# Holding five tiles of the last sequence back behind the last keys, moving their running sums to GpSimd, and reordering the work from the attention's biases to the end

## The reference

```
x = x + xattn(ln(x), ctx)     # 16 heads x 128; q, k = rmsnorm(x Wq), rmsnorm(ctx Wk); softmax(q k / sqrt(128)) (ctx Wv) Wo
x = x + attn(ln(x))           # 16 heads x 32, causal inside a sequence; qkv = x W + b, output W_proj + b
x = x + ffn(ln(x))            # silu(gate) * up, rms_norm, ternary weights: gate_up 512 -> 2 x 2048, proj 2048 -> 512
```

## Time and profile before

| | |
|---|---|
| three runs | 1558.96, 1561.87, 1562.70 us, median 1561.87 |
| profiled execution | 1560.27 us, its span 1558.4 us |
| mean granted TensorE clock | 0.985 of 2.4 GHz |
| TensorE busy | 1490.0 us, 96% of the span |
| VectorE, ScalarE, GpSimd busy | 1248.6, 970.6, 162.8 us |

### The profile page before, as it was taken

One profiled execution on the slowest core, in us unless ns is written; L12 is line 12 of the kernel. 1 busy time (PEld: TensorE's weight loads), 2 busy tenths in 40 slices (PEclk: granted clock), 3 DMA queues, 4 the chain that ended last, 5 costly groups with the idle time before them and its releaser, 6 DMA issues.

```text
span 1558.4 us, 21889 instructions
## 1 busy us (share of the span) xinstructions
PE 1490.0 (96%) x6860; PEld 1200.9 (77%) x6896; DVE 1248.6 (80%) x1952; ACT 970.6 (62%) x3637; POOL 162.8 (10%) x121
## 2 busy tenths in 40 slices
PE   7989999999999999999999999999999977987998
PEld 5767778888888888888888888888888855885786
DVE  6647878988898988899889889888988876768443
ACT  4666667767676767677667676776666654613332
POOL 2210000002000200110020002000202011022342
PEclk9999999999999999999999999999999988998999
DMA  5532221211221111112112111111110154450000
GB/s 175 172 116 71 68 70 45 65 42 32 78 68 35 60 58 60 43 57 67 51 31 80 56 46 55 58 46 39 51 30 20 44 178 135 149 217 1 1 0 28
DMA packets 86467, 105.19 MB, mean 67 GB/s; under 512 B 7240, under 2 KB 67664, under 8 KB 85328
## 3 DMA queue, kind: packets, MB, share of 16 engines
q1 hardware_dynamic: 79056, 96.46, 19.5%
q10 hardware_dynamic: 7296, 7.34, 1.4%
HBM read 81.24 MB, written 22.54 MB: 67 GB/s over the span
## 4 chain that ended last, share of the span: by engine, by line
PE 79%; DVE 13%; ACT 4%; issue 3%; DMA 1%; another core or an unknown queue 0%; POOL 0%; ACTq 0%; POOLq 0%; DVEq 0%
PE ps L36 25%; PE ps L37 24%; PE ps L38 24%; DVE ring L977 2%; PE ps L756 2%; PE ps L757 2%; ACT ps L1462 1%; DVE p_lo L42 1%; PE ps L774 1%; PE ps L775 1%; DVE ring L948 0%; ACT recip L1498 0%; DVE q_rstd L879 0%; DMA wq_raw<-in_wq 0%; DVE w_q L1062 0%
## 5 line engine op out<-in xcount | busy, mean ns | idle before, releaser
L1462 ACT ACTIVATE ps<-ps 123x128 f32<-123x128 f32 (+1 forms) x1248 | 325.5, 261 | 136.3 <-PE ps L38 135.5
L36 PE MATMUL ps<-wk_hi,cT_hi 128*128 128x512 f32 x832 | 330.1, 397 | 7.6 <-ACT ps L1462 4.4
L37 PE MATMUL ps<-wk_lo,cT_hi 128*128 128x512 f32 x832 | 326.9, 393 | 0.0
L38 PE MATMUL ps<-wk_hi,cT_lo 128*128 128x512 f32 x832 | 324.5, 390 | 0.0
L1462 ACT ACTIVATION_READ_ACCUMULATOR ps<-ps 123x1 f32 (+1 forms) x1248 | 231.1, 185 | 0.0
L36 PEld LDWEIGHTS ps<-wk_hi,cT_hi 128*128 128x128 f32 x832 | 156.4, 188 | 51.2 <-ACT ps L1462 10.7
L38 PEld LDWEIGHTS ps<-wk_hi,cT_lo 128*128 128x128 f32 x832 | 156.7, 188 | 34.4
L36 PE MATMUL ps<-p_hi,cn_hi 123*128 123x512 f32 (+1 forms) x416 | 173.2, 416 | 10.3 <-DVE p_lo L42 10.3
L37 PEld LDWEIGHTS ps<-wk_lo,cT_hi 128*128 128x128 f32 x832 | 157.0, 189 | 31.7
L37 PE MATMUL ps<-p_lo,cn_hi 123*128 123x512 f32 (+1 forms) x416 | 165.6, 398 | 0.0
L36 PE MATMUL ps<-fq_hi,cT_hi 128*128 128x512 f32 x416 | 162.2, 390 | 1.9 <-DVE fq_lo L42 1.9
(11 more groups left out here) (222 smaller groups left out, 2676.9 us busy)
## 6 DMA issues: line engine op xcount, KB each, us to landing
cT_raw<-in_ctxT SPq DMA_DIRECT2D x96, 128.0 KB, 3.5
cn_raw<-in_ctx SPq DMA_DIRECT2D x88, 123.0 KB
w_raw<-in_wguT SPq DMA_DIRECT2D x32, 256.0 KB, 2.7
qk_scratch<-folded ACTq DMA_DIRECT2D x8, 896.0 KB, 4.2
fq_raw<-qk_scratch SPq DMA_DIRECT2D x14, 512.0 KB, 3.7
pc_scratch<-pc_out SPq DMA_DIRECT2D x7, 1024.0 KB, 4.2
ternary_scratch<-w_out SPq DMA_DIRECT2D x48, 128.0 KB, 1.7
w_bf<-ternary_scratch SPq DMA_DIRECT2D x1, 6144.0 KB, 22.7
```

What stands on the lines that cost most here:

```text
L36: pe.matmul(dst, l_hi, r_hi, start=first, stop=False)
L37: pe.matmul(dst, l_hi, r_lo, start=False, stop=False)
L38: return pe.matmul(dst, l_lo, r_hi, start=False, stop=last)
L1462: done = act.activation(head, head, ACT.Square, accum_out=k_sum[0:n, i, g * GH + h:g * GH + h + 1])
```

## The change

1. **Steps.** The last key steps take one slot each; the program's loop ends at step N-1 = 103. Five tiles of the first part (94 to 98) have their context matmuls behind the last keys and scores, in a tail written out tile by tile; `cn_hi`/`cn_lo` get three buffers.
2. **GpSimd** takes the running sums of tiles 94 to 98 and the rescaling of the sum.
3. **Newton first.** Behind the last `key_mean` VectorE does `key_refine`, scale and maximum at once.
4. **End by halves of heads.** The sums, the reciprocal (`last_guess`, `last_refine`), the last tile's context (`last_context`) and `add_parts` go by half (8 heads); `divide_parts` of groups 1 to 3 lies in the head loop.
5. **Value loop.** Output matmuls are two heads behind (three `oT`, four `wo` buffers); the last three heads are ordered by token tile.
6. **Attention.** `qk_bias` goes to ScalarE; `low_wa(2, .)` lies ahead of `causal_shifted(1)`; `attend(m)` alternates banks 6 and 0.
7. **Feed-forward.** Gate and up of slice 1 for the first 256 tokens fill the place behind the last `z_turn`; the last slice's squares go to TensorE directly.

```diff
-        per_step = [0] * (TT + 1) + [1] * (LAST - TT) + [1, 1, 2, 2, 2, 2, 2, 1] + [1, 1, 2, 2, 2]
+        per_step = [0] * (TT + 1) + [1] * (LAST - TT) + [1, 1, 2, 2, 2, 2, 2, 1] + [1, 1, 1, 1]
+        HELD = slots_done[-1]
...
+        SUB_IN = {LAST: [LAST], LAST + 1: [LAST + 1], LAST + 2: [LAST + 2, LAST + 3], LAST + 3: [LAST + 4, LAST + 5]}
+        EXP_IN = {LAST: [LAST], LAST + 1: [LAST + 1], LAST + 2: [LAST + 2, LAST + 3], LAST + 3: [LAST + 4]}
...
+            def last_context():
+                v, n = N - 1, tiles[N - 1][2]
+                pe.wait_ge(p_lo_done, N)
+                denominators(v)
+                pe.wait_ge(cn_lo_done, N)
+                for half in range(2):
+                    hh = slice(half * BANK, (half + 1) * BANK)
+                    for c2 in range(KC):
+                        cc = slice(c2 * P, (c2 + 1) * P)
+                        done = products(pe, bank(PART_AV_BANK + c2 * 2 + half), cn_hi[0:n, v % 3, cc],
+                                        cn_lo[0:n, v % 3, cc], p_hi[0:n, v % 2, hh], p_lo[0:n, v % 2, hh], False, True)
+                    done.then_inc(av_mm, 1)
...
+            for half in range(2):
+                scores(N - 1, half)
+            for v in range(HELD - 1, N - 1):
+                for c2 in range(KC):
+                    weighted_context(v, c2)
+            last_context()
...
-                heads = [head - 1] if 1 <= head < H - 1 else [H - 2, H - 1] if head == H else []
+                late = range(H - NH3, H)
+                parts = [(m, [head - 2]) for m in range(MT)] if 2 <= head < H - 1 else [
+                    (0, late[:2]), (1, late[:2]), (0, late[2:]), (1, late[2:]), (2, late), (3, late)] if head == H else []
...
-                            pe.wait_ge(v_biased, MT)
-                            if m > 0:
-                                pe.wait_ge(aT_lo_done, m)
+                            pe.wait_ge(v_biased, max(m + 1, MT - 1))
+                            if m == 1:
+                                pe.wait_ge(causal_scaled, 4 * MT)
+                            elif m > 1:
+                                pe.wait_ge(aT_lo_done, m - 1)
...
             z_turn(MT - 1)
+            gate_or_up(1, 0, 0, 2)
+            gate_or_up(1, 1, 0, 2)
...
-            pe.wait_ge(h_sq_added, FT)
+            pe.wait_ge(h_sq_added, FT - 1)
+            pe.wait_ge(h_squared, FT)
...
+                pe.matmul(bank(7)[:, m:m + 1], sq_sum[:, cols], ones_col[:], start=True, stop=False)
+                done = pe.matmul(bank(7)[:, m:m + 1], h_sq[:, (FT - 1) % 2, cols], ones_col[:], start=False, stop=True)
...
-            sum_refine(B - 1)
-            add_parts()
-            evacuate(B - 1)
-            low_pc(0)
-            low_pc(1)
+            last_refine(0)
+            add_parts(0)
+            divide_parts(0)
+            add_parts(1)
+            low_pc(0)
+            add_parts(2)
+            add_parts(3)
+            low_pc(1)
+            last_refine(1)
...
+            def track_sum(u):
+                n = tiles[u][2]
+                pool.wait_ge(exped, u + 1)
+                pool.wait_ge(summed, sum_count(u - 1))
+                pool.tensor_tensor(run_sum[0:n], run_sum[0:n], ring[0:n, u % RING], ALU.add).then_inc(summed, 1)
+            track_sum(HELD - 1)
+            track_sum(HELD)
+            pool.wait_ge(maxed, max_count(N - 1))
+            pool.wait_ge(fq_lo_done, KC * B)
+            pool.partition_all_reduce(fq_raw[:], run_max[:], P, bass.bass_isa.ReduceOp.max).then_inc(max_spread, 1)
+            for u in range(HELD + 1, LAST + PART):
+                track_sum(u)
...
+            pool.tensor_tensor(run_sum[:], run_sum[:], col_max[:], ALU.mult).then_inc(sum_split, 1)
...
+            load_cn(HELD + 2)
+            sp.wait_ge(scores_mm, N)
+            sp.wait_ge(w_stored, 16 * NP)
+            load_v_weights(0)
+            load_v_weights(1)
+            for s in range(HELD + 3, N):
+                load_cn(s)
```

442 lines of the change are left out of this document (244 added, 198 removed).

## The result

The changed kernel takes 1548.28 us, median of 4 runs (1547.17 to 1548.97), against 1561.24 us of the kernel before, median of 4 on the same chip. The ratio is 0.9918, with a 95% interval of 0.99 to 0.9935: faster by 13 us. The profiled execution took 1548.61 us, 11.7 less than the one before; its span of 1545.9 is 12.5 shorter. So half of the forecast gain is missing, and the rest of this text looks for it.

What follows compares the result with a forecast made beforehand. TensorE, busy 1490.0 of 1558.4 us, bounds the kernel; only seams, mostly waits for VectorE with low clock behind long ones, can be won. Gains 11 + 1 + 1.5 + 8 + 2.5 + 1 = 25 us give 1535.3 us, range 1523 to 1549.

Steps and rivals of the forecast that it cites:

- B: Values: gain of 1 us (-1 to 3), with new small waits for the second and third head.
- C: Start of the attention: the 2.3 us wait shrinks by 0.7 us to all of it; gain 1.5 us (0.5 to 2.5).
- A: Tail, last keys to values: values start earlier; gain 11 us (3 to 20).
- Step 3: Tail, maximum to last `p_lo`: VectorE's own instructions take 24.5 us together.
- step 4: Tail: GpSimd and VectorE stand in each other's way, costing VectorE 10.2 us, 1.7 of them for the all-reduce.
- step 6: Tail: takes off 2 us for slow-clock matmuls behind remaining waits and 1 us for SP's queue.
- D: Attention: waits for `wa_lo` and `aT_lo` go, with the first's low clock; gain 8 us (4 to 10).
- E: Feed-forward start: 16 matmuls fill the 1.5 us wait and some clock comes back; gain 2.5 us (1 to 4).
- F: End: the 1.5 us wait for the last GpSimd addition goes, four one-column matmuls come; gain 1 us (0.5 to 1.5).
- rivals, 2: Tail, values and attention: gaps and low clock stay, the tail gains 3 us less; 1546 us, chance 0.19.
- Rival 3: Attention: the wait only changes its name, to `causal_scaled` and `p_diag`; gain there 2 us, 1541 us; chance 0.09.
- Rival 4: Tail: a GpSimd library load ahead of the all-reduce gates the maximum; 1571 us at a 30 us load; chance 0.05.

Runs made afterwards that it cites:

- Experiment 1: Changed kernel with the three divisions of groups 1 to 3 all behind the first head instead of one behind each of heads 1 to 3; 1544.19 us.
- experiments 1 and 2: The changed kernel with early divisions (1544.19 us), and the changed kernel with block 2's weights widened ahead of the loop over the feed-forward's slices (1548.23 us).
- Experiment 13: Experiment 11's kernel with the 16 query and key biases back on VectorE, in the order from before the change; 1541.78 us.
- Experiment 10: Experiment 6's kernel with all of attend's products in bank 6 again, as before the change; 1535.49 us.
- Experiment 11: Experiment 6's kernel with the old end: GpSimd adds the last slice's squares and TensorE multiplies only the sum; 1533.17 us.
- experiment 4: Changed kernel with context tiles 98 and 99 loaded ahead of the value and output weights in SP's queue; 1543.96 us.
- experiment 8: Experiment 5's kernel with two small GpSimd probe instructions, directly ahead of and behind the all-reduce; 1543.7 us.
- experiment 6: Experiment 5's kernel with block 2's weights widened ahead of the loop over the feed-forward's slices; 1535.14 us.
- experiment 5: Changed kernel with the running sums and rescaling back on VectorE and the three divisions behind the first head; 1536.39 us.
- kernels 5 to 12: The kernel with sums on VectorE and early divisions, and variants built on it; medians 1533.2 to 1536.4 us without the one with GpSimd probes.

## Why the prediction was wrong, step by step

**B is the step that failed most.** The prediction prices the values by the small waits of the second and third head and calls them a gain of 1 us. It looked at what the divisions (edit 4) displace on VectorE, and not at who waits for them: SP's store stands behind all four, and behind the store stand the weights and sums of the third group. With the divisions spread over the heads, the store went out 15.5 us behind the first value matmul, and B and C together lost 4.2 us where I forecast a gain of 2.5. Experiment 1 and the second column show it; with the divisions early the two stages gain 1.2 us.

**A was mis-sized.** Forecast 11; the profiled execution has 9.2. By the stretch from the last maximum to the values, the other executions with the same tail (the changed kernel again, experiments 1 and 2) are 1.5 to 3.0 us worse, so 6 to 9 us is the gain as a rule. Four of its steps can be set against the trace:

- Step 1 has the last keys end at 1239.4; they ended at 1240.99, 1.6 us late. Executions differ by up to 3.3 us there, so part of this is chance.
- Step 2 has 5.9 us from there to the maximum, and it took 6.2. The two sums ahead of it cost nothing that can be seen, as the step had it.
- Step 3 and the lock of step 4 have 34.7 us from the maximum to the last `p_lo`; it took 37.5, the same as before the change. The lock was right in mechanism and near in size: 7.6 us where 8.5 were forecast, 9.3 of 10.2 with the all-reduce. The rest is what the sum put at nothing: VectorE stood still for 3.7 us, 2.7 of them for tile 98, of which step 6 counts 1.
- Of the clock step 6 takes 2 us; it was 0.86 and 0.88 through the tail. What that cost cannot be read off, since VectorE and not TensorE sets most of the tail.

The sentence that "the move by itself costs more VectorE time than it saves" was right, and undersold: without the move the kernel is 6 us faster. I had nothing to set against it, and still gave A as 11, since the move was part of the change.

**C** (1.5) cannot be told apart from B: TensorE's wait for `yT_lo` is still 2.3 us in every kernel here, so the 0.7 us or more of it that I let go did not go.

**D was right in its sum and wrong in its split.** 8.0 of 8 in the profiled execution; the exact agreement is luck, as the same attention gives 5.3 to 9.5 us in the others. I gave 5.8 to the biases and 3.0 to the second bank. Experiment 13 gives the biases, with the order that goes with them, 7.6 us by the medians (6.8 by the traces). Experiment 10 gives the bank nothing that can be measured: behind the wait for `aT_lo` stood waits for `pT` on ScalarE, which take 2.1 us more in sum when it goes.

**E failed in the step "16 matmuls fill the wait".** Work put ahead of a wait is missing behind it. The 1.9 us had covered the way from slice 0's last product to the widened weights of `down(0)`; the wait for `zT_lo` of 1.5 us became one of 2.5 us with a slow clock behind it. In the profiled execution E lost 0.7 us instead of gaining 2.5. The slow clock is not always there: where it stayed at 1.00 behind the wait, the stretch from the first gate matmul to the end takes 99.1 us instead of 100.8, and E and F together gain 1.3. With the widening first it takes 97.3 us, against 100.4 before the change, 3.1 of the 3.5 us that I forecast for E and F.

**F** gained 0.3 of 1. The wait of 1.5 us went, but in its place stand an issue of 0.3, 16 one-column matmuls for 8 (0.9 us more) and a slower start of the last products. Experiment 11 shows no loss without it.

Of the rivals, 2 comes nearest in time (1546), and its reason is true only in part. Its sign is there in the tail, with the clock at 0.86 and 0.88; the other losses are there because the change made new waits, not because the old ones were kept. Rival 3's wait for `sc` or `p_diag` did not come; a wait did change its name there, to `pT`, and D held all the same. Rival 4's pause exists, with 7 to 12 us instead of the 25 that it needed: between the second sum and the end of the maximum lay 10.05 us, and the all-reduce started 0.14 us behind the maximum.

The range holds the measured 1548.28 us, at its upper end, by a slip in the sum: half of each of the bounds of A to F gives 1527 to 1544, and 1523 to 1549 takes about three quarters of each.

What stays open: why the clock falls behind a given wait in one execution and not in the next, and with it 1 to 4 us of any single trace; what the pause behind the all-reduce costs through the place of the four additions; why the median of experiment 4 is 4 us lower when its trace shows only a wait that moved; and the 2.2 us for `pc_lo` ahead of the first value matmul, which stand in every kernel behind the change and were not tried.

## What to carry to other kernels

When an instruction is moved later to free its engine, list everything that waits for it on the other queues, the DMA queue above all: a store that waits for the last of four pieces is as late as the last piece, and so is everything queued behind it. When work is moved ahead to fill a wait, look at the next wait behind its old place and what it covered there. And when a shared port makes two engines take turns, an addition moved to the slower of them can cost the faster one more than doing it itself: here up to 2.2 us of stretching for 1.14 us saved. Work kept on the busy engine can also fill its own waits: two sums of 1.14 us each took most of a wait of 2.7 us.

## What the runs showed of the hardware

- GpSimd needs 7.2 to 11.65 us when it changes between an all-reduce and ordinary arithmetic, with no instruction in the trace; with everything ready it is 10.12 us ahead of the all-reduce and 7.18 us behind it (experiment 8). Its length varies from run to run of the same code (8.64, 9.03 us in two executions of the changed kernel).
- A GpSimd addition of 2.39 us holds up even a VectorE instruction on 16 columns for its whole length: 2.39 us instead of 0.17 (changed kernel, 1234.79).
- Behind the same wait of 2.5 us ahead of `down(0)` the granted clock was 0.72 over the next 6 us in the changed kernel, and 1.00 in its second execution.
- The same attention, with nearly the same waits, took 73.0 to 77.2 us. In the kernel of experiment 6 the granted clock was 0.79 in 1360.2 to 1368.2 and 0.70 in 1408.2 to 1416.2; in that of experiment 5 it was 1.00 in both. So a single trace cannot price a change in the attention to better than 2 to 4 us, and the medians of kernels 5 to 12 without the probes (1533.2 to 1536.4) do not rank them.
